# A graph layer with layer norm: the first block of M moved ahead of the c products, r on half columns, and one of the last normalisations given to VectorE

## The chip, the cores and the metric

One core of one Trainium2 chip. The metric is the device time of one execution in microseconds, the median of several runs. Names of engines: TensorE (PE; PEld are its weight loads), VectorE (DVE), ScalarE (ACT), GpSimd (POOL), and SyncE (SP), which here only issues loads and stores.

## The reference

`x` is 128 graphs of 64 nodes with 384 features (8192 tokens), `adj` a 64 x 64 matrix of 0 and 1 for each graph. Cut to what matters:

```
dep_emb = dep_emb_table[adj]
hi = x @ W1[:384] + dep_emb @ W1[384:] + b1          # for each pair i, j
hj = x @ W2[:384] + dep_emb @ W2[384:] + b2
relevance = sum(hi * hj, -1)
A = softmax(where(adj != 0, relevance, -1e9), axis=2)
h = relu((A @ x) @ gcn_w + gcn_b)
out = layernorm(x + h @ Wo + bo)
```

Where `adj` is 1 everywhere that counts, the embedding is one fixed row (type 1), so with c1 = emb[1] @ W1[384:] + b1 and c2 likewise, relevance is a bilinear form in x: x_i M x_j, with M = W1[:384] W2[:384]^T, plus x_i . u with u = W1 c2, plus x_j . r with r = W2 c1, plus k = c1 . c2. The kernel computes this, and at the end looks whether an entry of `adj` is over 1; only then does it run a second, general program, which these inputs don't need.

## The kernel before, in words

The tokens are worked in 16 groups of 512 (four tiles of 128 tokens, `q` 0 to 3). The loop over the groups is written out as a pipeline: `body(g, par)` runs for each group on every engine, the first two and the last two groups with their indices fixed. In a group TensorE mixes (`mix`, L523), forms scores (`score_stage`, L468), values of the next group (`value`), the output product of the group before (L544 to L550), a transpose (L503) and the projection of the next group (`proj`). Large products are made in three parts from a high and a low half (`three`, L444 to L446). Each engine's order is written out by hand in its own block of the program, and semaphores join them: `x.then_inc(s, 1)` raises `s` when x is done, and `wait_ge(s, n)` holds the engine, with all that is queued behind, until it has that value.

The change lies in two places. The first is the start:

- TensorE, once VectorE has cleared `zero`, multiplies zeros (`warm`, L557) with the widths in `WARM_UP`. Then it computes c1 and c2 (L569: six products from `edge_sb`, 64 columns each, into two PSUM banks), one more product of zeros of width `FILL`, and M (L579): for each of three blocks c of the sum, three products d of 128 x 385 that add into three banks. The first 384 columns are M, the last, column `HID` of `w2t_sb`, is c2, so that u comes out with M. M waits for the loads of w1 and w2 (`w12_loaded[c]`) and, ahead of block 0, for `c2_ready`.
- r follows (`r_stage`, L587): three columns of 128, each a sum of three products whose weights are 128 columns of `w2t_sb` and whose moving operand is c1, repeated over 64 columns, into `score`. Then L595 lays gcn_b out over all rows (`gb_diag` times ones, into `GB_BANK`), and the value products of group 0 begin. Behind the first of them stands the small product for k (L599).
- VectorE copies the embedding, waits for `bias_loaded` and `c_mm`, writes c2 into column `HID` of `w2t_sb` (L893), writes `c2_sb` and `c1_sb`, then `gb_diag`, c1 * c2, the low halves of x (L907) and of gcn_w (L911), u's low half (L914), and the copy of gcn_b's row (L917), then M's low halves.
- ScalarE issues the loads of the embedding, w1, the biases and gcn_w, and makes the high halves (L770 to L784). SyncE issues the loads of w2 (L378) and x. GpSimd makes the identity and part of the low halves of x.

The second place is the end, the last group (`LAST`, 15). For each of its four tiles VectorE adds x, takes the statistics (L864) and the moments (L873); GpSimd adds eps and takes the power -1/2 (`inverse_std`, L1152 and L1154); for tiles 0 to 2 GpSimd also computes the shift (`shift`, L1161) and ScalarE normalises with it (`normalise_last`, L763), after which SyncE stores the tile (L422). Tile 3 is normalised by VectorE from PSUM (L1035), and ScalarE issues its store (L828). Between its moments and that, VectorE computes the flag of the general program (L1030, L1032). `normalise` (L881) is VectorE's form from SBUF, used in the groups before.

## Time and profile before

| | us |
|---|---|
| runs | 382.44, 381.17, 382.26 |
| median | 382.26 |
| the profiled execution, its own time | 382.89 |
| its span, first to last instruction | 380.8 |
| TensorE busy in it | 373.4 |
| VectorE busy | 218.5 |
| GpSimd busy | 153.3 |
| ScalarE busy | 142.5 |

The profile is of one execution. The views used are the page (busy time of each engine, the chain of work that ended last, followed back from the last instruction), the timeline (start and length of instructions in order), the chain of waits in a stretch, the tables by source line, and the busy time by stretch with the granted clock of TensorE as a share of 2.4 GHz. Times are us from the start of the span. A product on float32 data stands as two records, a weight load and a product each; a row with "x12" merges twelve of them. In brackets stands how long the engine had stood idle, and what ended that.

### The profile page before, as it was taken

The numbers are of one execution on the slowest core, as the hardware profiler recorded it, in microseconds if no ns is written. First come the engines' busy times: TensorE is split into PE (matmuls) and PEld (weight loads), VectorE is DVE, ScalarE is ACT, GpSimd is POOL, SyncE is SP. The second block draws the span as 40 slices with busy tenths as digits, with TensorE's granted clock in tenths as the row PEclk, the third lists the DMA queues.
The fourth block names the chain that finished last, engine by engine and source line by source line (L and its number), as shares of the span: only waits on it lengthen the run. The fifth ranks groups of instructions, "written<-read, shape, count | busy, mean of one in ns | idle before, by whom it ended". The sixth has DMA issues, their size and how long they took to land.

```text
span 380.8 us, 10033 instructions
## 1 busy us (share of the span) xinstructions
PE 373.4 (98%) x3983; PEld 342.3 (90%) x3983; DVE 218.5 (57%) x582; ACT 142.5 (37%) x343; POOL 153.3 (40%) x134
## 2 busy tenths in 40 slices
PE   8999999999999999999999999999999999999993
PEld 5789898998989899898989989898998989898993
DVE  1534265665646566464756646476664647666594
ACT  1724541523434152343414234341523435133343
POOL 0332545080724508072450807235080723608034
PEclk9999999999999999999999999999999999999998
DMA  7922022608053170715317071431707143170105
GB/s 231 318 102 84 16 83 45 221 2 226 37 166 98 29 233 0 218 44 147 114 27 234 0 209 53 139 123 22 239 0 209 52 133 129 26 240 0 45 27 184
DMA packets 34851, 42.88 MB, mean 113 GB/s; under 512 B 10128, under 2 KB 29072, under 8 KB 34832
## 3 DMA queue, kind: packets, MB, share of 16 engines
q1 hardware_dynamic: 33600, 41.13, 35.7%
q10 hardware_dynamic: 1232, 1.49, 1.2%
q8 instruction: 13, 0.21, 0.2%
q14 instruction: 6, 0.05, 0.0%
HBM read 30.03 MB, written 12.58 MB: 112 GB/s over the span
## 4 chain that ended last, share of the span: by engine, by line
PE 91%; DVE 4%; DMA 1%; POOL 1%; ACT 1%; issue 0%; ACTq 0%; POOLq 0%
PE banks L444 18%; PE banks L446 18%; PE banks L445 18%; PE banks L544 7%; PE banks L550 7%; PE banks L545 7%; PE banks L523 6%; PE banks L468 6%; PE banks L579 2%; DMA bias_sb<-in_biases_dram 1%; DVE stats L864 1%; PE banks L503 1%; POOL rstd L1154 1%; DVE y_sb L859 1%; DVE hs_lo L942 1%; PE banks L587 1%
## 5 line engine op out<-in xcount | busy, mean ns | idle before, releaser
L1143 POOL TENSOR_TENSOR x_sb<-x_sb,wob_sb 128x1536 f32<-128x1536 f32 x15 | 52.8, 3519 | 175.9 <-DVE weights L973 162.8
L942 DVE SCALAR_TENSOR_TENSOR hs_lo<-banks,hs_hi 128x256 fp32r<-128x256 f32 x90 | 32.5, 416 | 67.3 <-ACT hs_hi L804 67.2
L444 PE MATMUL banks<-gcn_hi,xt_hi 128*128 128x386 f32 x192 | 66.9, 348 | 0.0
L446 PE MATMUL banks<-gcn_hi,xt_lo 128*128 128x386 f32 x192 | 64.9, 338 | 0.0
L445 PE MATMUL banks<-gcn_lo,xt_hi 128*128 128x386 f32 x192 | 64.8, 338 | 0.0
L544 PE MATMUL banks<-wo_hi,hs_hi 128*128 128x384 f32 x180 | 60.9, 338 | 0.0
L550 PE MATMUL banks<-wo_hi,hs_lo 128*128 128x384 f32 x180 | 60.5, 336 | 0.0
L545 PE MATMUL banks<-wo_lo,hs_hi 128*128 128x384 f32 x180 | 60.5, 336 | 0.0
L745 ACT ACTIVATE gt_sb<-banks,r_sb 128x512 f32<-128x512 f32 x48 | 33.0, 688 | 71.5 <-PE banks L446 71.4
L444 PE MATMUL banks<-xt_hi,m_hi 128*128 128x512 f32 x144 | 57.4, 398 | 0.0
L446 PE MATMUL banks<-xt_hi,m_lo 128*128 128x512 f32 x144 | 56.8, 394 | 0.0
L445 PE MATMUL banks<-xt_lo,m_hi 128*128 128x512 f32 x144 | 56.4, 392 | 0.0
L1134 POOL TENSOR_TENSOR xt_lo<-xt_sb,xt_hi 128x1536 fp32r<-128x1536 f32 x15 | 52.8, 3521 | 0.7 <-ACT xt_hi L739 0.7
L859 DVE TENSOR_TENSOR y_sb<-banks,x_sb 128x384 f32<-128x384 f32 x60 | 33.3, 555 | 28.4 <-PE banks L550 28.4
L849 DVE TENSOR_TENSOR hg_sb<-banks,gb_row 128x385 f32<-128x385 f32 x64 | 34.4, 554 | 23.0 <-PE banks L446 23.0
L444 PEld LDWEIGHTS banks<-gcn_hi,xt_hi 128*128 128x128 f32 x192 | 36.3, 189 | 1.2
L445 PEld LDWEIGHTS banks<-gcn_lo,xt_hi 128*128 128x128 f32 x192 | 36.3, 189 | 0.2
L794 ACT ACTIVATE prob<-rel,nmax 128x64 f32<-128x64 f32 x64 | 21.5, 337 | 39.5 <-DVE nmax L961 39.5
L446 PEld LDWEIGHTS banks<-gcn_hi,xt_lo 128*128 128x128 f32 x192 | 36.3, 189 | 0.0
L864 DVE BATCH_NORM_STATS2 stats<-y_sb 128x6 f32<-128x384 f32 x60 | 33.6, 560 | 2.0
L544 PEld LDWEIGHTS banks<-wo_hi,hs_hi 128*128 128x128 f32 x180 | 33.9, 188 | 0.2
L545 PEld LDWEIGHTS banks<-wo_lo,hs_hi 128*128 128x128 f32 x180 | 33.8, 188 | 0.1
(97 smaller groups left out, 516.0 us busy)
## 6 DMA issues: line engine op xcount, KB each, us to landing
xt_sb<-in_x_t_dram SPq DMA_DIRECT2D x15, 768.0 KB, 4.5
x_sb<-in_x_dram SPq DMA_DIRECT2D x15, 768.0 KB, 5.6
out_dram<-y_sb SPq DMA_DIRECT2D x30, 384.0 KB, 5.8
adj_sb<-in_adj_dram SPq DMA_DIRECT2D x32, 64.0 KB, 2.2
xt_sb<-in_x_t_dram SPq DMA_DIRECT2D x2, 384.0 KB, 8.4
xt_sb<-in_x_dram SPq DMA_DIRECT2D x1, 768.0 KB, 4.7
w1t_sb<-in_w_t_dram ACTq DMA_DIRECT2D x3, 192.0 KB, 5.4
w2t_sb<-in_w_t_dram SPq DMA_DIRECT2D x3, 192.0 KB, 4.5
```

Of the source, the lines that this page charges most:

```text
L444: pe.matmul(acc, a_hi, b_hi, start=first, stop=False)
L445: pe.matmul(acc, a_hi, b_lo, start=False, stop=False)
L446: return pe.matmul(acc, a_lo, b_hi, start=False, stop=last)
L544: pe.matmul(acc, hs_home(g)[0][:, c, ts], wo_hi[:, c, :], start=opens, stop=False)
L545: pe.matmul(acc, hs_home(g)[0][:, c, ts], wo_lo[:, c, :], start=False, stop=False)
L550: mm = pe.matmul(out_bank(g, q)[:, 0:HID], hs_home(g)[1][:, c, ts], wo_hi[:, c, :], start=False, stop=(c == BLOCKS[-1]))
L849: dve.tensor_tensor(hg_sb[:, slot, q, :], VALUE_BANK[q][:, 0:HID + 1], gb_row[:], ALU.add).then_inc(hg_ready, 1)
L859: dve.tensor_tensor(y_home(g, slot)[:, q, :], out_bank(g, q)[:, 0:HID], x_home(g, slot)[:, q, :], ALU.add).then_inc(added, 1)
L864: dve.bn_stats(stats[:, q, :], y_home(g, slot)[:, q, :]).then_inc(statd, 1)
L942: a = dve.scalar_tensor_tensor(by_graph(hs_home(g)[1][:, f, :])[:, h], mixed(f)[:, h], 0.0, by_graph(f32(hs_home(g)[0][:, f, :]))[:, h], A ...
L1134: pool.tensor_tensor(xt_lo[:, slot], xt_sb[:, slot], f32(xt_hi[:, slot]), ALU.subtract).then_inc(xlo, 1)
L1143: pool.tensor_tensor(x_home(g, slot), x_home(g, slot), wob_sb[:].rearrange("p (o n) -> p o n", o=1).to_broadcast([P, PAIRS, HID]), ALU.add ...
```

## The change

In words:

- `WARM_UP` becomes three products of 384 columns (were 384, 384, 128), and the filler product behind the c products goes.
- M's first block (`m_stage(0)`) comes right behind the warm-up. It waits for its loads and for `zero_column`: VectorE sets the column `HID` of block 0 of `w2t_sb` to 0 (its second instruction), so that the block adds nothing to u.
- The c products follow, then the row of gcn_b, now in bank 2. Behind them six products with one column each (weights: 64 columns of `w1t_sb` block 0; moving: `c2_sb[:, 0:1]`) add block 0's part of u into column `HID` of M's banks. They wait for both c2 writes. Then come M's blocks 1 and 2.
- r's products are cut into halves of 64 weight columns each, 18 in place of nine.
- VectorE writes `gb_diag` ahead of its wait for the c products, and copies gcn_b's row ahead of the low halves of x. As bank 2 is the second value product's, that product waits for `gb_row_ready`.
- In the last group GpSimd's shift and ScalarE's normalisation go for tile 2. VectorE normalises it from SBUF right behind tile 3's moments, ahead of the flag. SyncE's store of it and ScalarE's store of tile 3 wait for `y_ready` with the counts that belong to that.

TensorE, start of the program, before (names: `edge_sb` holds embedding and its weights, `c_sb` are c1 and c2):

```order
L557 MATMUL banks<-zero 128x384 [waits warm_zero]
L557 MATMUL banks<-zero 128x384
L557 MATMUL banks<-zero 128x128
L569 MATMUL banks<-edge_sb 128x64 [waits emb_ready,edge_loaded1,edge_loaded0]
L569 MATMUL banks<-edge_sb 128x64 x5
L557 MATMUL banks<-zero 128x128
L579 MATMUL banks<-w2t_sb,w1t_sb 128x385 [waits c2_ready,w12_loaded0]
L579 MATMUL banks<-w2t_sb,w1t_sb 128x385 x2
L579 MATMUL banks<-w2t_sb,w1t_sb 128x385 [waits w12_loaded1]
L587 MATMUL banks<-c_sb,w2t_sb 128x64 [waits c1_ready]
L587 MATMUL banks<-c_sb,w2t_sb 128x64 x8
L595 MATMUL banks<-gb_diag,ones 128x384 [waits gb_diag_ready,ones_ready]
```

The same place after the change:

```order
L560 MATMUL banks<-zero 128x384 x2
L571 MATMUL banks<-w2t_sb,w1t_sb 128x385 [waits w12_loaded0,zero_column]
L571 MATMUL banks<-w2t_sb,w1t_sb 128x385 x2
L592 MATMUL banks<-edge_sb 128x64 [waits emb_ready,edge_loaded1,edge_loaded0]
L592 MATMUL banks<-edge_sb 128x64 x5
L597 MATMUL banks<-gb_diag,ones 128x384 [waits gb_diag_ready,ones_ready]
L603 MATMUL banks<-c_sb,w1t_sb 64x1 [waits c2_ready]
L603 MATMUL banks<-c_sb,w1t_sb 64x1 x5
L571 MATMUL banks<-w2t_sb,w1t_sb 128x385 [waits w12_loaded1]
L581 MATMUL banks<-c_sb,w2t_sb 64x64 [waits c1_ready]
L581 MATMUL banks<-c_sb,w2t_sb 64x64 x17
```

M's first block has moved ahead of the c products, and between them and M's second block stand the row of gcn_b and six products of one column.

VectorE, end of the program, before:

```order
L1025 BN_STATS stats<-banks 128x6 [waits out_mm]
L873 BN_AGGR mv<-stats 128x2 [waits statd]
L1030 TENSOR_REDUCE all_max<-banks 1x1 [waits rowmax_mm]
L1032 TENSOR_SCALAR general<-all_max 1x1 [waits allmax_ready]
L1035 TENSOR_SCALAR xt_sb<-banks,mv,rstd 128x384 [waits rstd_ready]
```

and after:

```order
L1041 BN_STATS stats<-banks 128x6 [waits out_mm]
L887 BN_AGGR mv<-stats 128x2 [waits statd]
L895 TENSOR_SCALAR xt_sb<-xt_sb,mv,rstd 128x384 [waits rstd_ready]
L1047 TENSOR_REDUCE all_max<-banks 1x1 [waits rowmax_mm]
L1049 TENSOR_SCALAR general<-all_max 1x1 [waits allmax_ready]
L1052 TENSOR_SCALAR xt_sb<-banks,mv,rstd 128x384 [waits rstd_ready]
```

The row of L895 is tile 2's normalisation, and the maximum, the flag and tile 3's normalisation now stand behind it.

```diff
@@ -47,8 +47,7 @@
 P = 128
 NEG = 1.0e9
 EPS = 1e-5
-WARM_UP = 384, 384, 128
-FILL = 128
+WARM_UP = 384, 384, 384
 
 
 def gnn_layernorm_kernel(nc, x, x_t, adj, adj_t, edge, biases, w1_t, w2_t, gcn_w, wo_w, wo_b, out):
@@ -175,8 +174,8 @@
         PROJ0_BANK = bank[5:8]
         PROJ1_BANK = [bank[5], bank[2], bank[3]]
         C_BANK = bank[3], bank[4]
+        GB_BANK = bank[2]
         ROWMAX_BANK = bank[4]
-        GB_BANK = bank[4]
         BLOCKS = 0, 2, 1
         K_AT = C * NODES
 
@@ -206,6 +205,7 @@
         ident_zero = sem("ident_zero")
         ident_ready = sem("ident_ready")
         warm_zero = sem("warm_zero")
+        zero_column = sem("zero_column")
         attn_zero = sem("attn_zero")
         ones_ready = sem("ones_ready")
         c_mm = sem("c_mm")
@@ -418,7 +418,10 @@
             sp.dma_start(x_sb[:, 1], x_rows[1]).then_inc(x_loaded[1], 16)
             run(sp, body)
             for q in range(PAIRS - 1):
-                sp.wait_ge(y_end, q + 4)
+                if q < HALVES:
+                    sp.wait_ge(y_end, q + 4)
+                else:
+                    sp.wait_ge(y_ready, HALVES * (LAST - 1))
                 sp.dma_start(out_rows[LAST][:, q], y_home(LAST, 1)[:, q]).then_inc(stored[1], 16)
             again = is_general(sp)
 
@@ -561,6 +564,26 @@
             for n in WARM_UP:
                 warm(n)
 
+            def m_stage(c):
+
+                pe.wait_ge(w12_loaded[c], 32)
+                for d in range(C):
+                    mm = pe.matmul(M_BANK[d][:, 0:HID + 1], w1t_sb[:, c, d * P:(d + 1) * P], w2t_sb[:, c, :],
+                                   start=(c == 0), stop=(c == C - 1))
+                    if c == C - 1:
+                        mm.then_inc(m_mm, 1)
+
+            def r_stage(d):
+
+                for c in range(C):
+                    for e in range(2):
+                        at = d * P + e * NODES
+                        pe.matmul(score[e * NODES:(e + 1) * NODES, d * NODES:(d + 1) * NODES],
+                                  w2t_sb[:, c, at:at + NODES], c1_sb[:, c:c + 1].to_broadcast([P, NODES]),
+                                  start=(c == 0), stop=(c == C - 1))
+
+            pe.wait_ge(zero_column, 1)
+            m_stage(0)
             for n in range(2):
                 pe.wait_ge(edge_loaded[n], 16)
             pe.wait_ge(emb_ready, 1)
@@ -569,35 +592,26 @@
                     mm = pe.matmul(C_BANK[n][:, c * NODES:(c + 1) * NODES], w[:, c * P:(c + 1) * P],
                                    emb[:, 1:2].to_broadcast([EDIM, NODES]), start=True, stop=True)
             mm.then_inc(c_mm, 1)
-            warm(FILL)
-
-            for c in range(C):
-                pe.wait_ge(w12_loaded[c], 32)
-                if c == 0:
-                    pe.wait_ge(c2_ready, 1)
-                for d in range(C):
-                    mm = pe.matmul(M_BANK[d][:, 0:HID + 1], w1t_sb[:, c, d * P:(d + 1) * P], w2t_sb[:, c, :],
-                                   start=(c == 0), stop=(c == C - 1))
-                    if c == C - 1:
-                        mm.then_inc(m_mm, 1)
-
-            def r_stage(d):
-
-                for c in range(C):
-                    pe.matmul(score[:, d * NODES:(d + 1) * NODES], w2t_sb[:, c, d * P:(d + 1) * P],
-                              c1_sb[:, c:c + 1].to_broadcast([P, NODES]), start=(c == 0), stop=(c == C - 1))
-
-            pe.wait_ge(c1_ready, 1)
-            for d in range(C):
-                r_stage(d)
             pe.wait_ge(ones_ready, 1)
             pe.wait_ge(gb_diag_ready, 1)
             pe.matmul(GB_BANK[:, 0:HID], ones[:].to_broadcast([P, P]), gb_diag[:],
                       start=True, stop=True).then_inc(gb_mm, 1)
+            pe.wait_ge(c2_ready, 2)
+            for d in range(C):
+                for e in range(2):
+                    at = d * P + e * NODES
+                    pe.matmul(M_BANK[d][e * NODES:(e + 1) * NODES, HID:HID + 1], w1t_sb[:, 0, at:at + NODES],
+                              c2_sb[:, 0:1], start=False, stop=False)
+            m_stage(1)
+            m_stage(2)
+            pe.wait_ge(c1_ready, 1)
+            for d in range(C):
+                r_stage(d)
             value(0, 0, 0)
             pe.wait_ge(c12_sb_ready, 1)
             pe.matmul(score[:, K_AT:K_AT + C], ones[:].to_broadcast([P, P]), c12_sb[:],
                       start=True, stop=True).then_inc(rk_mm, 1)
+            pe.wait_ge(gb_row_ready, 1)
             value(0, 0, 1)
             pe.wait_ge(m_lo_ready, C)
             pe.wait_ge(xlo, 1)
@@ -822,9 +836,9 @@
             normalise_last(LAST - 2, 1, 1, (2, 3))
             normalise_last(LAST - 1, 0, 2, (0, 1))
             normalise_last(LAST - 1, 0, 3, (2, 3))
-            for q in range(PAIRS - 1):
+            for q in range(HALVES):
                 normalise_last(LAST, 1, q + 4, (q,))
-            act.wait_ge(y_ready, HALVES * (LAST - 1))
+            act.wait_ge(y_ready, HALVES * (LAST - 1) + 1)
             act.dma_start(out_rows[LAST][:, PAIRS - 1], y_home(LAST, 1)[:, PAIRS - 1]).then_inc(stored[1], 16)
 
             with act.If(is_general(act)):
@@ -883,24 +897,28 @@
                 a.then_inc(y_ready, 1)
 
             dve.memset(zero[:], 0.0).then_inc(warm_zero, 1)
+            dve.memset(w2t_sb[:, 0, HID:HID + 1], 0.0).then_inc(zero_column, 1)
             dve.memset(attn[:], 0.0).then_inc(attn_zero, 1)
             dve.memset(ones[:], 1.0).then_inc(ones_ready, 1)
             dve.memset(adj_max[:], 0).then_inc(max_zero, 1)
             dve.wait_ge(edge_loaded[0], 16)
             dve.tensor_copy(emb2_sb, emb1_sb).then_inc(emb_ready, 1)
             dve.wait_ge(bias_loaded, 16)
-            dve.wait_ge(c_mm, 1)
-            dve.tensor_tensor(w2t_sb[:, :, HID], C_BANK[1][:, 0:C * NODES:NODES], b2_sb, ALU.add).then_inc(c2_ready, 1)
-            dve.tensor_tensor(c2_sb[:], C_BANK[1][:, 0:C * NODES:NODES], b2_sb, ALU.add).then_inc(c2_ready, 1)
-            dve.tensor_tensor(c1_sb[:], C_BANK[0][:, 0:C * NODES:NODES], b1_sb, ALU.add).then_inc(c1_ready, 1)
             dve.memset(gb_row[:, HID:HID + 1], 0.0)
             dve.wait_ge(ident_ready, 1)
             for c in range(C):
                 a = dve.tensor_scalar(gb_diag[:, c * P:(c + 1) * P], ident[:], gb_sb[:, c:c + 1], None, ALU.mult)
             a.then_inc(gb_diag_ready, 1)
+            dve.wait_ge(c_mm, 1)
+            dve.tensor_tensor(w2t_sb[:, 1:C, HID], C_BANK[1][:, NODES:C * NODES:NODES], b2_sb[:, 1:C],
+                              ALU.add).then_inc(c2_ready, 1)
+            dve.tensor_tensor(c2_sb[:], C_BANK[1][:, 0:C * NODES:NODES], b2_sb, ALU.add).then_inc(c2_ready, 1)
+            dve.tensor_tensor(c1_sb[:], C_BANK[0][:, 0:C * NODES:NODES], b1_sb, ALU.add).then_inc(c1_ready, 1)
             dve.wait_ge(c2_ready, 2)
             dve.wait_ge(c1_ready, 1)
             dve.tensor_tensor(c12_sb[:], c1_sb[:], c2_sb[:], ALU.mult).then_inc(c12_sb_ready, 1)
+            dve.wait_ge(gb_mm, 1)
+            dve.tensor_copy(gb_row[:, 0:HID], GB_BANK[:, 0:HID]).then_inc(gb_row_ready, 1)
 
             for c in range(C):
                 dve.wait_ge(xt0_hi, c + 1)
@@ -913,8 +931,6 @@
                 dve.wait_ge(u_hi_ready, c + 1)
                 dve.tensor_tensor(gcn_lo[:, c, HID:HW], M_BANK[c][:, HID:HID + 1].to_broadcast([P, 2]),
                                   f32(gcn_hi[:, c, HID:HW]), ALU.subtract).then_inc(u_lo_ready, 1)
-            dve.wait_ge(gb_mm, 1)
-            dve.tensor_copy(gb_row[:, 0:HID], GB_BANK[:, 0:HID]).then_inc(gb_row_ready, 1)
             for d in range(C):
                 dve.wait_ge(m_hi_ready, d + 1)
                 dve.tensor_tensor(m_lo[:, d, :], M_BANK[d][:, 0:HID], f32(m_hi[:, d, :]),
@@ -1025,6 +1041,7 @@
             dve.bn_stats(stats[:, q, :], out_bank(LAST, q)[:, 0:HID]).then_inc(statd, 1)
             dve.wait_ge(statd, PAIRS * GROUPS)
             moments(LAST, (q,))
+            normalise(LAST, 1, PAIRS - 1, (2,))
 
             dve.wait_ge(rowmax_mm, 1)
             dve.tensor_reduce(all_max[:], ROWMAX_BANK[0:1, 0:P], AX_X, ALU.max).then_inc(allmax_ready, 1)
@@ -1201,7 +1218,7 @@
             run(pool, body)
             for q in range(PAIRS):
                 inverse_std(LAST, q, slice(q, q + 1))
-                if q < PAIRS - 1:
+                if q < HALVES:
                     shift(LAST, q, (q,))
 
             with pool.If(is_general(pool)):
```

## Rows read from the trace of the kernel before

**Rows 1.** The page: busy time by engine, and the chain that ended last by engine.
```profile
PE 373.4 (98%) x3983; PEld 342.3 (90%) x3983; DVE 218.5 (57%) x582; ACT 142.5 (37%) x343; POOL 153.3 (40%) x134
...
PE 91%; DVE 4%; DMA 1%; POOL 1%; ACT 1%; issue 0%; ACTq 0%; POOLq 0%
```
**Rows 2.** Chain of waits from 4 to 18.8 us: start, length, what.
```profile
1.95 4.59 DMA bias_sb<-in_biases_dram
...
6.87 7.52 PE banks L579 x18
14.39 1.95 PE banks L587 x18
16.34 0.70 PE banks L595 x2
```
**Rows 3.** Timeline of TensorE up to M: start, length, engine, line, operation.
```profile
0.92 3.35 PE L557 MATMUL banks<-zero 128*128 128x384 f32 x6 [0.92 <-DVE zero L885]
4.21 1.55 PE L569 MATMUL banks<-edge_sb 64*128 64x64 f32 x12
5.68 0.79 PE L557 MATMUL banks<-zero 128*128 128x128 f32 x2
```
**Rows 4.** Busy time and granted clock of one stretch (PEclk before the DMA share).
```profile
0.00:4.00 4.00, 3.08 (x6) 1.85 (x6) 0.90 (x5) 0.00 (x0) 0.94 (x9) 1.00 0.45 131
```
**Rows 5.** Timeline of TensorE's weight loads in M, one record each.
```profile
7.64 0.33 PEld L579 LDWEIGHTS banks<-w2t_sb,w1t_sb 128*128 128x128 f32 x1 [0.31 <-issue]
...
9.56 0.32 PEld L579 LDWEIGHTS banks<-w2t_sb,w1t_sb 128*128 128x128 f32 x1 [0.30 <-issue]
10.02 0.19 PEld L579 LDWEIGHTS banks<-w2t_sb,w1t_sb 128*128 128x128 f32 x1
10.67 0.19 PEld L579 LDWEIGHTS banks<-w2t_sb,w1t_sb 128*128 128x128 f32 x1
```
**Rows 6.** w2's loads: their issue, and the first one's time to landing.
```profile
1.52 1.63 SPq L378 DMA_DIRECT2D w2t_sb<-in_w_t_dram  x3
...
w2t_sb<-in_w_t_dram SPq DMA_DIRECT2D x1, 192.0 KB, 4.8
```
**Rows 7.** Chain of waits: the first score stage.
```profile
29.81 1.55 PE banks L468 x48
```
**Rows 8.** Weight loads of r and of a score stage, ns min/median/max.
```profile
L587 PEld LDWEIGHTS banks<-c_sb,w2t_sb x18: 190/192/192, 13.9 to 16.0; 128*128 128x128 f32 x18
...
L468 PEld LDWEIGHTS banks<-xt_sb,gt_sb x48: 132/138/138, 29.7 to 31.1; 128*64 128x64 f32 x48
```
**Rows 9.** Timeline of VectorE at the start.
```profile
11.57 1.09 DVE L907 TENSOR_TENSOR xt_lo<-xt_sb,xt_hi 128x256 fp32r<-128x256 f32 x3 [4.05 <-ACT xt_hi L770]
...
17.08 0.56 DVE L917 COPY gb_row<-banks 128x384 f32<-128x384 f32 x1 [2.07 <-PE banks L595]
```
**Rows 10.** Timeline behind the last product, on VectorE, GpSimd and ScalarE's queue.
```profile
375.22 0.18 DVE L873 BATCH_NORM_AGGREGATE mv<-stats 128x2 f32<-128x6 f32 x1
375.32 0.25 DVE L1030 TENSOR_REDUCE all_max<-banks 1x1 f32<-1x128 f32 x1
375.46 0.27 POOL L1161 TENSOR_SCALAR nmr<-mv,rstd 128x1 f32<-128x1 f32 x1
375.60 0.14 DVE L1032 TENSOR_SCALAR general<-all_max 1x1 int32<-1x1 f32 x1
375.69 0.19 POOL L1152 TENSOR_TENSOR veps<-mv,eps_sb 128x1 f32<-128x1 f32 x1
...
375.96 0.55 POOL L1154 TENSOR_TENSOR rstd<-veps,mhalf 128x1 f32<-128x1 f32 x1
376.54 0.68 DVE L1035 TENSOR_SCALAR xt_sb<-banks,mv,rstd 128x384 f32<-128x384 f32 x1 [0.80 <-POOL rstd L1154]
377.25 0.37 ACTq L828 DMA_DIRECT2D out_dram<-xt_sb  x1
```
**Rows 11.** VectorE's normalisations from SBUF, ns min/median/max.
```profile
L881 DVE TENSOR_SCALAR y_sb<-y_sb,mv,rstd x54: 446/474/480, 61.9 to 351.4; 128x384 f32<-128x384 f32 x54
```

## The prediction, made before the changed kernel was run

> **What bounds the kernel now.** I read the page first. TensorE is busy 98% of the span and the chain that ended last is 91% TensorE [rows 1], so between the first and the last product nothing but TensorE's own stream counts: time put into it or taken out of it arrives at the end. What is left is the stretch before the stream is dense and the stretch behind it. So I read the chain of waits over the first 19 us [rows 2]. It runs from the bias load, which lands at 1.95 + 4.59 = 6.54, over two small VectorE operations into M, which starts at 6.87 and lasts 7.52, then r (1.95), the row of gcn_b (0.70), and from 17.04 on the dense value products. In the timeline of TensorE ahead of it [rows 3] stand the warm-up until 4.27, the c products until 5.76 and the one filler product until 6.47: all three are spent waiting for the bias and for w2's first block, so none of them costs anything now.
>
> Then the clock. The granted clock reads 1.00 from the start [rows 4], but the records say otherwise: a product on float32 data has two records, and the weight loads of M that begin at 7.64 and 9.56 are three records apart, 0.64 us each; the next follows after 0.46, at 10.02, and two later it is 10.67, 0.32 each [rows 5]. 385 columns in 0.64 and in 0.32 are the 1.2 GHz and the 2.4 GHz level, so I go by the spacing and not by the granted clock, which has no record of the start. If the 0.46 is part slow and part fast, the rise is at 9.56 + 0.28 = 9.84. TensorE had then been busy since 0.92 but for 0.4 us ahead of 6.87, with the small c products in the middle.
>
> The tail I read in the timeline [rows 10]. VectorE's last normalisation waits for rstd, which GpSimd ends at 375.96 + 0.55 = 376.51, and GpSimd was kept by the shift of the third tile.
>
> **M's first block.** It no longer waits for the bias but for the zero column and for w1 and w2. w2's block is issued at 1.52 and lands 4.8 later, at 6.32 [rows 6]; M can start at 6.39 in place of 6.87, 0.48 earlier. The longer warm-up has two products with 256 more columns each, 0.43 us more apiece at 0.64 per 384 columns: it ends at 4.27 + 0.86 = 5.1, still ahead of 6.32, so it costs nothing, and TensorE stands idle for 1.3 us behind it. If the clock rises at 9.84 as before, the six records of the block start at 6.39, 7.16, 7.80, 8.44, 9.08 and 9.72 (first gap 0.77, as 6.87 to 7.64 before) and end at 10.10; before, the sixth ended at 10.34. **Term: -0.24.**
>
> **The c products.** Twelve records take 5.68 - 4.21 = 1.47 [rows 3]. They used to lie in the wait for the loads; now they lie behind M's first block, on the path. r's records with the same 64 columns go at the fast clock in (16.34 - 14.22) / 18 = 0.118 each, against 0.122 here, so the clock doesn't change their price; 0.1 less is the lower end. **Term: +1.47.** The filler leaves with no effect, as it was in the wait.
>
> **The row of gcn_b** moves from behind r to behind the c products: 0.65 to 0.7 either way [rows 2]. It covers most of the way from the last c product over two VectorE operations to c2, which took 0.33 between bias and M [rows 2]. Term: 0. Its copy on VectorE (0.56) now stands ahead of xt_lo (1.09 for three) [rows 9], which so start at about 13 and end at 14.2; the first value product, which wants them, comes at about 17.8. Covered by 3 us; with no cover the most is the whole 0.56. The wait of the second value product for gb_row ends 5 us before it.
>
> **The six products that add u's first block**, twelve records with one moving column and 64 weight columns: nothing like it is in the trace. Nearest is the score stage, 48 records of 64 x 64 that alternate between the two column halves, in 1.55 [rows 7], 0.032 each: 0.39. The other end is r's record now, 0.118: 1.4. Below 0.4 it can't well go, as the records must be issued on a busy engine. The form is the score stage's, so I take 0.4 and 0.1 for getting under way. **Term: +0.5**, range +0.4 to +1.4.
>
> **r on half columns.** 18 products of 64 x 64 in place of nine of 128 x 64, 36 records. At the score stage's rate 36 x 0.032 = 1.16, in place of 2.12. **Term: -0.96**; the other end is 0 or a little over, if two half products take as long as a whole one. What bounds the whole ones is that the weights of the next (0.192 alone) and a short product take turns [rows 8]. The Trainium skill (TensorE: Matmul & The Clock Gate, Part 3, on what overlaps) has weight loads overlap with running products only where the row group differs, and here every product uses all rows. By that rule column halves would win nothing over r as it is, and the sum would be 1.0 higher. The score stage alternates column halves with all rows in use and still goes at 0.032 a record while one of its weight loads lasts 0.138 [rows 7, 8]: the loads do overlap, and the row decides.
>
> Before M's end the chain over ScalarE's u_hi and VectorE's u_lo has to be ready for the first value product. Today r's 2.12 covers it, and no wait shows; with 1.16 the cover is thinner. What follows M's last product there is two ScalarE copies and two VectorE subtractions, the longest of them no longer than the 0.56 of the gcn_b copy, and they overlap in pairs; I take it to stay hidden, and give it 0.3 in the upper end.
>
> **The tail.** GpSimd leaves out the third tile's shift (0.27). The last rstd then waits for the moments of tile 3, at 375.22 + 0.18 = 375.40, in place of 375.69: veps 0.19 and rstd 0.55 with 0.16 between gives 376.3 in place of 376.51 [rows 10]. VectorE takes the third tile's normalisation, 0.47 [rows 11], ahead of the maximum and the flag (0.42 together): 375.40 + 0.47 + 0.42 = 376.3 as well. So the last normalisation starts 0.2 earlier, and with it the last store, issued at 377.25. **Term: -0.2**, range -0.3 to +0.2 (VectorE the later one). The third tile's own store goes out earlier, at about 375.9, and is not last.
>
> **Sum:** -0.24 + 1.47 + 0.5 - 0.96 - 0.2 = +0.57. The profiled execution took 382.89 (span 380.8), so its like would take 383.46. That execution is 0.63 above the median of the runs shown, 382.26; on the median I forecast **382.8**. A measurement of this kernel can tell about 0.3%, 1.15 us, from no change; the forecast lies inside.
>
> **Rivals.**
> 1. *The clock rises before M's first block.* The warm-up is now one piece of full-width products until 5.1, where it ended at 4.27 and the small c products followed. If that brings the clock up, the block's six records take 6 x 0.32 and some 0.1, 2.0 in place of 3.71: 1.7 less, **381.1**. For it: the three runs shown spread over 1.27 us, about the price of some slow records, as if the rise fell differently in them. Against it: the 1.3 us of idle behind the warm-up, and that nearly unbroken work from 0.92 to 6.47 did not bring it up before M in the trace [rows 3, 5]. The spread of the runs weighs enough for a chance of 0.35. The Trainium skill (the same page, Part 1, on what is happening) calls the point of the rise variable from run to run, because the monitor does not start with the kernel; the spread would agree, and one trace alone can't show it.
> 2. *The clock rises later.* The c products and the u products, small in columns, now stand in the middle of M. If they break up the activity before the rise, the row of gcn_b (0.65 more) and three records of M's second block (0.32 more each) go at the slow level: +1.6, **384.4**. It decides when the rise would otherwise have come after 10.1. Against it: M's first block is dense from 6.39 on, as M was from 6.87 when the clock rose at 9.84. Chance 0.10.
> 3. *Column halves don't run side by side.* r costs 2.1 as now, and u's records 0.118 each: 0.96 + 0.9 more, **384.7**; with r alone, 383.8. Against it stand the 48 records of the score stage. Chance 0.08.
> 4. The forecast's own case, rise at about 9.84: 0.47.
>
> **How the numbers follow.** Rival 1 at 381.1 lies just at the bound of 0.3% (381.1), and with the scatter of a median some two thirds of it is told as faster: 0.23, and 0.04 for a cheaper path than I see: faster 0.27. Slower (above 383.4) are rivals 2 and 3 and a tenth of the forecast's case, where u or the tail are at their upper ends: 0.23. The rest, 0.50, is within 0.3%. The range 380.8 to 384.0 takes in rival 1 with some scatter, the forecast's case with u at its upper end (+0.9), and r alone without a gain; outside are most of rival 2 and the whole of rival 3. The forecast's own case spans 382.2 to 383.8.
>
> **What would show it.** M's first weight load at 6.35; its records 0.64 apart until about 9.8, or 0.32 from the start (rival 1); c products from about 10.1; M's second block at 12.7 (its loads have landed by then); r in 1.2; the first value product at 17.8 in place of 17.04; the end of TensorE's stream 0.8 later; the last normalisation 0.2 nearer to the last product. I am wrong in the mechanism if the value products start before 17.0 with the clock rising at 9.8 or later, or if r takes more than 1.6.

## The result, and the profile after

| | us |
|---|---|
| changed kernel, six runs | 379.76 to 380.41, median 379.96 |
| kernel before, six runs beside it | 381.17 to 383.34, median 382.31 |
| ratio | 0.9944, 95% interval 0.9924 to 0.9964 |
| the changed kernel's profiled execution, its own time | 380.05 |
| its span | 378.0 |

The change makes the kernel faster by 0.56%, about 2.1 us. I had forecast 382.8 with a range of 380.8 to 384.0: no change, where there is a clear gain, and 379.96 lies below the range.

The page of the changed kernel, busy time and the chain, against [rows 1]:

```profile
PE 372.1 (98%) x4011; PEld 340.0 (90%) x4011; DVE 220.7 (58%) x584; ACT 142.1 (38%) x342; POOL 153.3 (41%) x133
...
PE 98%; DVE 0%; POOL 0%; issue 0%
```

The chain is now TensorE's from the warm-up on: no load and no VectorE operation bounds the start of this execution. The chain of waits from 3 to 18 us, against [rows 2]:

```profile
2.56 2.56 PE banks L560 x4
5.12 2.79 PE banks L571 x6
7.91 0.81 PE banks L592 x12
8.72 0.84 PE banks L597 x2
9.56 0.45 PE banks L603 x12
10.01 4.08 PE banks L571 x12
14.09 1.20 PE banks L581 x36
15.29 0.38 PE banks L447
```

In this order stand the warm-up, M's first block, the c products, the row of gcn_b, u's six products, M's other blocks, r, and the first value product at 15.29, where it was at 17.04. So the value products begin 1.75 us earlier. About 0.2 of that is lost at once, as the first of them takes 0.38 where it took 0.17; TensorE's last product starts 1.66 earlier (374.42 before, 372.76 after). That is the start's part of the difference of 2.8 between the two spans. The weight loads of M's first block, against [rows 5]:

```profile
5.00 0.50 PEld L571 LDWEIGHTS banks<-w2t_sb,w1t_sb 128*128 128x128 f32 x2 [1.03 <-issue]
5.81 0.33 PEld L571 LDWEIGHTS banks<-w2t_sb,w1t_sb 128*128 128x128 f32 x1 [0.31 <-issue]
6.45 0.20 PEld L571 LDWEIGHTS banks<-w2t_sb,w1t_sb 128*128 128x128 f32 x1 [0.31 <-issue]
6.78 0.19 PEld L571 LDWEIGHTS banks<-w2t_sb,w1t_sb 128*128 128x128 f32 x1
```

5.81 to 6.45 is 0.64, the 1.2 GHz level; 6.45 to 6.78 is 0.33, the 2.4 GHz level. The clock rose at about 6.45, not at 9.84.

The other 1.2 us lies behind the last product. The timeline of the tail, against [rows 10]:

```profile
373.57 0.18 DVE L887 BATCH_NORM_AGGREGATE mv<-stats 128x2 f32<-128x6 f32 x1
373.77 0.48 DVE L895 TENSOR_SCALAR xt_sb<-xt_sb,mv,rstd 128x384 f32<-128x384 f32 x1
...
374.10 0.56 POOL L1171 TENSOR_TENSOR rstd<-veps,mhalf 128x1 f32<-128x1 f32 x1
...
374.47 0.14 DVE L1049 TENSOR_SCALAR general<-all_max 1x1 int32<-1x1 f32 x1
374.69 0.68 DVE L1052 TENSOR_SCALAR xt_sb<-banks,mv,rstd 128x384 f32<-128x384 f32 x1
375.40 0.37 ACTq L842 DMA_DIRECT2D out_dram<-xt_sb  x1
```

From the moments to the last normalisation it is 1.12 (373.57 to 374.69), where it was 1.32: the 0.2 of the forecast. But from the issue of the last store to the end of the span it is 2.6, where it was 3.55. The transfers from that issue on, before and then changed: in each the bandwidth in 40 slices, the queues that carry instructions, and the last store with its time to landing.

```profile
GB/s 0 266 369 430 328 328 369 348 144 41 0 321 287 307 348 369 389 328 267 171 0 0 0 20 0 20 0 0 20 0 20 20 20 20 21 0 0 0 0 0
...
q8 instruction: 1, 0.02, 2.0%
...
out_dram<-xt_sb ACTq DMA_DIRECT2D x1, 192.0 KB, 3.1
```

```profile
GB/s 354 354 402 307 190 24 0 0 0 0 0 0 0 165 307 354 378 378 354 354 378 189 142 0 24 126 252 0 0 0 0 0 0 0 0 0 0 0 0 0
...
q8 instruction: 1, 0.02, 2.4%
...
out_dram<-xt_sb ACTq DMA_DIRECT2D x1, 192.0 KB, 2.1
```

Before, the store's data are almost all moved by the twentieth slice (1.5 us behind the issue), and then, after a gap, single rows (20 GB/s in a slice) follow for some 0.9 us. In the changed kernel that trickle is missing. A packet of instructions, 16 KB, stands beside the store in both. Its place is what the first group of experiments turns on.

### The profile page after: what moved, and what is told of

Read it like the earlier page. It is cut to its first block, busy times and chain, and to the rows that moved or that the text cites. A ratio compares the mean times of both kernels' runs of the same rounds, so it can differ in the third digit from the quotient of the medians.

```text
span 378.0 us, 10088 instructions
## 1 busy us (share of the span) xinstructions
PE 372.1 (98%) x4011; PEld 340.0 (90%) x4011; DVE 220.7 (58%) x584; ACT 142.1 (38%) x342; POOL 153.3 (41%) x133
## 4 chain that ended last, share of the span: by engine, by line
PE 98%; DVE 0%; POOL 0%; issue 0%
PE banks L447 18%; PE banks L449 18%; PE banks L448 18%; PE banks L547 9%; PE banks L548 9%; PE banks L553 9%; PE banks L526 7%; PE banks L471 7%; PE banks L571 2%; PE banks L560 1%; PE banks L506 1%; PE banks L581 0%; PE banks L597 0%; PE banks L592 0%; DVE xt_sb L1052 0%; PE banks L540 0%
## 6 DMA issues: line engine op xcount, KB each, us to landing
out_dram<-y_sb SPq DMA_DIRECT2D x30, 384.0 KB, 5.8
xt_sb<-in_x_t_dram SPq DMA_DIRECT2D x2, 384.0 KB, 8.4
```

## The experiments

Sixteen kernels ran, in four series, each on another chip. The kernel before was timed 29 to 35 times in each series. These times fall into two groups: in the first series 16 from 380.45 to 381.47 and 13 from 382.09 to 382.95, in the others 17, 20 and 20 in the lower one and 18 (from 381.94), 15 (from 382.31) and 14 (from 382.01) in the upper. I call them its early and its late group; the part on the start says why.

| kernel | median | of the kernel before, same series | ratio (95% interval) |
|---|---|---|---|
| after_old_tail | 381.36 | 381.23 | 0.9996 (0.9981 to 1.0011) |
| after_whole_r | 380.39 | 381.23 | 0.9977 (0.9958 to 0.9995) |
| after_short_warm | 381.23 | 381.23 | 0.9984 (0.9963 to 1.0005) |
| after_again | 379.57 | 381.94 | 0.9949 (0.9930 to 0.9968) |
| after_c_first | 379.55 | 381.94 | 0.9946 (0.9923 to 0.9968) |
| after_flag_first | 381.00 | 381.94 | 0.9974 (0.9955 to 0.9994) |
| before_long_warm | 381.39 | 381.94 | 1.0002 (0.9981 to 1.0024) |
| before_flag_last | 380.99 | 381.28 | 0.9972 (0.9948 to 0.9995) |
| before_new_tail | 379.69 | 381.28 | 0.9968 (0.9947 to 0.9989) |
| before_half_r | 380.71 | 381.28 | 0.9972 (0.9953 to 0.9991) |
| after_flag_last | 379.92 | 381.28 | 0.9965 (0.9941 to 0.9989) |
| after_third | 380.05 | 381.16 | 0.9969 (0.9947 to 0.9991) |
| start_only | 381.99 | 381.16 | 1.0012 (0.9990 to 1.0034) |
| after_longer_warm | 380.24 | 381.16 | 0.9966 (0.9947 to 0.9984) |
| row_loaded | 379.28 | 381.16 | 0.9947 (0.9924 to 0.9969) |

before_again was one execution, 380.75. The median of a kernel with two groups jumps with a few runs from one to the other, so I compare groups where I can.

### The tail

**after_old_tail.** The changed kernel with the tail of before:

```diff
-            normalise(LAST, 1, PAIRS - 1, (2,))
...
-                if q < HALVES:
+                if q < PAIRS - 1:
                     shift(LAST, q, (q,))
```

with ScalarE's normalisation of tile 2 and the waits of the two stores as before.

> The changed kernel with the tail of before (ScalarE normalises tile 2 behind GpSimd's shift). Theory A (in the tail the change wins only the 0.2 us by which the last normalisation comes nearer to the last product; that the last store landed 1.0 us sooner behind its issue is chance): 380.2, 0.2 over the changed kernel's 380.0. Theory B (the store lands sooner because the stores before it went out sooner): 381.1, and the last store takes 3.1 us to land again.

Measured: 381.36, and the last store takes 3.1 again. The three series that have the changed kernel have it at 0.9944, 0.9949 and 0.9969 of the kernel before; without the new tail it is at 0.9996. So the tail is worth 1.0 to 2.0 us, not 0.2, and the store's landing is no chance. Theory B of this run had the effect right but named the wrong cause, as the next runs show.

**after_flag_first and before_flag_last.** The same four lines (the maximum over `adj` and the flag of the general program), moved in opposite directions:

```diff
+            dve.tensor_scalar(general[:], all_max[:], 1.0, None, ALU.is_gt).then_inc(general_ready, 1)
             normalise(LAST, 1, PAIRS - 1, (2,))
```

is the first, the changed kernel with the flag ahead of tile 2. The second is the kernel before with the flag behind tile 3:

```diff
                               ALU.subtract, ALU.mult).then_inc(y_ready, 1)
+            dve.tensor_scalar(general[:], all_max[:], 1.0, None, ALU.is_gt).then_inc(general_ready, 1)
```

> The changed kernel with the maximum and the flag ahead of tile 2's normalisation on VectorE, as early as in the kernel before. Theory A (an instruction load of 16 KB follows the flag by 2.3 to 2.8 us in every trace so far; with the early flag it falls into the last store's packets and holds up the last nine of them): the last store takes 3.1 us to land in place of 2.1, and the median is 0.7 to 1.0 above the changed kernel. Theory B (the store lands sooner because tile 2's store went out sooner): 2.1 again, and no difference.

> The kernel before with the maximum and the flag moved behind tile 3's normalisation on VectorE; nothing else. Theory A (the load of instructions that follows the flag is what holds up the last store): the last store lands 2.0 to 2.1 us behind its issue in place of 3.1 to 3.6, and the median is 0.8 to 1.3 below the kernel before, with its two groups still there. Theory B (the new tail's gain needs tile 2's earlier store): 3.1 again, no difference.

Measured: after_flag_first has its runs from 380.56 to 381.52, median 381.00, 1.4 above the changed kernel of the same series. Its last store and the transfers behind 375.5:

```profile
GB/s 355 410 341 355 137 0 146 0 0 68 259 341 396 355 192 27 73 0 14 14 0 14 14 14 27 14 0 0 0 0 0 0 0 0 0 0 0 0 0 0
...
out_dram<-xt_sb ACTq DMA_DIRECT2D x1, 192.0 KB, 3.1
```

The trickle is back, with tile 2's store as far ahead of the last one as in the changed kernel: its issue ends 0.79 us before the last one's begins in both. In before_flag_last the trickle is gone, and tile 2's store is as close to the last one as in the kernel before (0.42 in both):

```profile
GB/s 382 369 205 301 369 328 410 314 55 0 0 0 0 287 410 369 341 287 55 0 273 355 341 396 301 82 0 0 0 0 0 0 0 146 73 0 0 0 0 0
...
out_dram<-xt_sb ACTq DMA_DIRECT2D x1, 192.0 KB, 1.9
```

Its four lowest runs are 379.43 to 379.85, where the early group of the kernel before begins at 380.49, and the other eight are 380.97 to 381.56, where the late group begins at 382.31: both groups are lower, by 1.1 and 1.3 at their lowest runs. The flag's place alone is worth that. The packet of instructions says how: it starts 2.34 us behind the flag in the kernel before (375.74 to 378.08) and 2.51 in the changed one (374.61 to 377.12), and 2.0 to 2.8 in all traces. Before, this falls into the store's packets, here with the last column the share of the sixteen engines' time in 0.2 us:

```profile
q8 instruction: 1, 0.02, 30.0%
q10 hardware_dynamic: 13, 0.02, 26.7%
```

(the kernel before, 378.0 to 378.2), while in the changed kernel, from 377.0 to 377.2, one packet of the store is left:

```profile
q8 instruction: 1, 0.02, 30.6%
q14 instruction: 1, 0.01, 15.8%
q10 hardware_dynamic: 1, 0.00, 0.2%
```

The share gives the packet's length: 30.0% of sixteen times 0.2 us is 0.96 us. So in the kernel before the instruction packet is done at 379.04, and the last rows of the store begin at 379.03. The same holds in all seven traces with an early flag: the last eight rows begin to move within 0.02 us of the packet's end, and the store lands 1.3 us behind that end. Where the packet took longest (before_long_warm, 44.8% of 0.2 us, so 1.43 us), the store did too, 3.6. Over all eighteen traces, the store lands 3.1 to 3.6 behind its issue in the seven with an early flag, and 1.9 to 2.2 in the eleven with a late one. That some engine of the DMA handles both and serves them in turn is what I conclude from these times; the traces don't name the engine.

**before_new_tail.** The kernel before with the four edits of the new tail.

> The kernel before with the changed tail alone. Theory A: the flag is late enough as a side effect, the store lands in 2.0 to 2.1, and the last normalisation comes 0.2 nearer: 1.0 to 1.5 below the kernel before, two groups still there. Theory B (the tail is worth the 0.2 that I forecast): 0.2 below.

Measured: eight runs from 378.78 to 379.94 and four from 381.19 to 381.84, the groups 1.7 and 1.1 below those of the kernel before at their lowest runs, with the store at 2.0. Theory A. The new tail is worth about 1.3: in the traces 1.1 of it is the store's landing (3.1 to 2.0), the side effect that VectorE comes to the flag later, and 0.2 the effect that I had priced. The runs can't tell that 0.2 from nothing: before_flag_last, which lacks it, is as far below the kernel before (ratios 0.9972 and 0.9968).

**after_flag_last.** The changed kernel with the flag behind tile 3's normalisation.

> The changed kernel with the flag behind tile 3's normalisation. Theory A (the later load of instructions is clear of the store by more, but the branch over the general program ends later by about 0.7): the store lands in 2.0 to 2.1 as in the changed kernel, and the time is within 0.3 of it. Theory B (the flag ahead of the last normalisation costs VectorE time on the path): 0.2 to 0.5 below the changed kernel.

Measured: nine runs from 379.16 to 380.26, three from 381.80 to 382.30. The changed kernel did not run in this series; in the others its lower runs lie from 379.16 to 380.84, and so do these nine. The store lands in 1.9. No more shows than with the flag between the two normalisations. Theory A.

### r

**after_whole_r and before_half_r** exchange the halved products of r for the whole ones, in the changed kernel and in the one before:

```diff
-                    for e in range(2):
-                        at = d * P + e * NODES
-                        pe.matmul(score[e * NODES:(e + 1) * NODES, d * NODES:(d + 1) * NODES],
+                    pe.matmul(score[:, d * NODES:(d + 1) * NODES], w2t_sb[:, c, d * P:(d + 1) * P],
```

> The changed kernel with r on whole columns again. Theory A (36 records in 1.20 us side by side in place of 18 in 2.12, all of it on the path): 380.9, 0.9 more. Theory B (r covers the chain to u's low half, or something behind it waits anyway): 380.0 to 380.4.

> The kernel before with r on half columns alone. Theory A (on the path in full): r takes 1.2 in place of 2.1 and the median falls by 0.9. Theory B (the row of gcn_b or u's low half, which r covered, is waited for instead): 0.2 to 0.6 less, and an idle stretch of TensorE behind r.

Measured: whole r has 11 of 12 runs from 379.92 to 380.75, median 380.39, a ratio of 0.9977 against 0.9944 to 0.9969 for the changed kernel: 0.3 to 1.3 us more. Half r in the kernel before gives 380.71 to 381.28, ratio 0.9972. Here the late group comes down by the full 0.8 (its lowest runs 381.52, against 382.31), but the early one by 0.4 only (380.06 against 380.49). The trace suggests why the halves differ. It is an early execution, and M ran into its own loads, as the chain of waits from 4 us on has it:

```profile
2.43 6.62 DMA w1t_sb<-in_w_t_dram
...
9.09 4.15 PE banks L579 x12
13.24 1.20 PE banks L589 x36
```

r itself takes 1.20 in place of 1.95 to 2.1. The wait that appears is not B's, but one for w1's second block, which landed 6.6 us behind its issue in this trace; one trace doesn't show how often that happens. Nor is the price quite Theory A's 0.9. In the chain r gets 0.75 shorter (1.95 to 1.20), the row of gcn_b behind it 0.14 longer (0.70 to 0.84), and from M's end to the second value product it is 0.62 less than in the kernel before (2.83 to 2.21). The traces of after_whole_r and the changed kernel differ by 0.60 in the same stretch. So r is worth about 0.6.

### The start and the clock

**before_again**, the kernel before unchanged:

> The kernel before, unchanged, for a second trace. Theory A (two loads landed late by chance in the first trace, w2's first block 4.8 us and the bias 4.6 us behind their issue, where the changed kernel's trace has 3.4 and 3.1): here they land about 3.3 behind their issue again in many executions, M starts near 5.9, behind the filler product, and the time is about 381.3. Theory B (the landing belongs to the kernel's own order of work): M starts at 6.87 again, and the time is about 382.5.

Measured: 380.75, and a chain that differs from [rows 2] in two ways:

```profile
1.94 3.91 DMA bias_sb<-in_biases_dram
...
6.18 6.06 PE banks L579 x18
12.24 1.95 PE banks L587 x18
...
14.90 0.18 PE banks L444
```

The bias landed 0.7 earlier, so theory A is half right: the landing varies. The more important difference is that M takes 6.06 in place of 7.52. Its weight loads and those of the c products:

```profile
4.19 0.97 PEld L569 LDWEIGHTS banks<-edge_sb 64*128 64x128 f32 x12 [0.23 <-issue]
...
6.15 5.47 PEld L579 LDWEIGHTS banks<-w2t_sb,w1t_sb 128*128 128x128 f32 x18 [0.62 <-DMA w2t_sb<-in_w_t_dram]
```

18 loads in 5.47 are 0.32 apart from the first: the clock was up before M, from the c products on (0.97 for twelve where it was 1.36). Without any change in the code the first value product comes at 14.90 in place of 17.04. These are the two groups. The traces of the kernel before and of its variants bear it out: the clock is up before M in before_again (380.75), before_new_tail (379.10) and before_half_r (380.92), all in the lower group of their kernel; it rises only in M's first block, at 9.5 or later, in the first trace (382.89), before_flag_last (381.19) and before_long_warm (383.65), all in the upper one. The Trainium skill (TensorE: Matmul & The Clock Gate, Part 1, on what is happening) says that the point of the rise varies from run to run. The six traces agree, but not with the page's size of it, 500 ns either way: by the spacing of the records the clock is up by 4.1 us in before_new_tail, and not before 9.7 in before_long_warm.

**before_long_warm.** The longer warm-up and no filler product, in the kernel before:

```diff
-WARM_UP = 384, 384, 128
-FILL = 128
+WARM_UP = 384, 384, 384
```

> The kernel before with the longer warm-up (three times 384) and without the filler product. Theory A (the length of the dense stretch sets how often the clock rises before M): the slow group of the kernel before, near 382.5, thins out or goes, and the median comes down by about 0.5 or more. Theory B (only the order with M's block behind the warm-up does it): both groups stay as they are.

Measured: 381.39, ratio 1.0002, three of twelve runs at 383.16 or more, where the kernel before has 18 of 35 in its late group. With twelve runs that is a hint of fewer late rises, no proof. Its late runs are later still: its trace has M from 7.03, and the loads 0.64 apart until 9.73.

**after_short_warm.** The changed kernel with the old warm-up, 384, 384, 128.

> The changed kernel with the warm-up of before (384, 384, 128 columns). Theory A (the longer warm-up is what brings the clock up at 6.5, in the middle of M's first block): with 0.86 us less of it the rise comes a good deal later, all six records of the first block, the c products, the row of gcn_b and part of the second block run at the slow level, 381.5 to 382.5. Theory B (the rise follows from M's first block coming early and close behind the warm-up, and not from the warm-up's length): 380.0, with M at 5.0 either way.

Measured: two groups again, five runs from 379.55 to 380.16 and seven from 381.00 to 382.19. Five are as good as the changed kernel; the others are late. The trace is one of those:

```profile
5.95 0.33 PEld L571 LDWEIGHTS banks<-w2t_sb,w1t_sb 128*128 128x128 f32 x1 [0.31 <-issue]
6.59 0.34 PEld L571 LDWEIGHTS banks<-w2t_sb,w1t_sb 128*128 128x128 f32 x1 [0.31 <-issue]
...
7.88 0.34 PEld L571 LDWEIGHTS banks<-w2t_sb,w1t_sb 128*128 128x128 f32 x1 [0.30 <-issue]
```

M's first block starts at 5.18, as in the changed kernel, and runs at the slow level nearly to its end. TensorE had stood idle for 0.9 us from 4.27 on. Theory A: with the shorter warm-up seven of twelve runs are late, and B is out, as M began equally early. The whole set of kernels with the changed start and the long warm-up (the changed kernel, after_old_tail, after_whole_r, after_flag_first, after_flag_last and start_only) has 8 late runs of 90. The run doesn't tell whether the longer work counts or the smaller gap behind it, for both changed. A gap need not cost the clock: in start_only the warm-up ended at 4.58, TensorE waited 1.62 us for w2, and M's first block ran at the fast level throughout:

```profile
6.20 2.18 PE L568 MATMUL banks<-w2t_sb,w1t_sb 128*128 128x385 f32 x6 [1.62 <-DMA w2t_sb<-in_w_t_dram]
```

**after_longer_warm.** Four warm-up products.

> The changed kernel with four warm-up products in place of three: the fourth ends at 6.4 at the slow level, or at 5.8 to 6.1 where the clock has risen by then. Theory A (the rise needs dense work ahead of it and what is lost is the delay of M's first block): no slow run, narrower scatter, M's first block at 5.8 to 6.4 mostly at the fast level, and a median 0 to 0.6 above the changed kernel. Theory B (the rise does not depend on the warm-up): 0.8 to 1.3 above, the whole delay of M.

Measured: 379.27 to 380.90, median 380.24, against 380.05 for after_third beside it, which has two runs at 382.15 and 382.16. No late run, and 0.2 more. Theory A. Twelve runs without a late one are no proof against 8 of 90, and the intervals of the two kernels overlap.

**after_again and after_third**, the changed kernel unchanged:

> The changed kernel, unchanged, beside the others of this call. Theory A (the clock's rise falls differently in each execution, and a dense warm-up until 5.1 lets it fall between about 4.5 and 7.0 every time): runs within 1 us of one another, no second group, while the kernel before falls into two groups about 1.7 us apart. Theory B (the change moves one fixed rise): both kernels scatter alike. The median is about 1.2 below the kernel before of the same call by either; the last store lands 2.1 us behind its issue.

> The changed kernel once more, as the measure for the other three of this call: about 379.6 to 380.0, with at most one run in twelve 1.5 or more above the rest.

Measured: 379.16 to 380.47 in twelve runs, then ten from 379.32 to 380.84 and two at 382.15. With the first six that is 2 late runs of 30, where the kernel before had 60 of 133 in the four series. I had expected none in the first of the two and at most one in the second; the second has two.

**after_c_first.** The c products ahead of M's first block, all else as changed:

```diff
-            pe.wait_ge(zero_column, 1)
-            m_stage(0)
...
             mm.then_inc(c_mm, 1)
+            pe.wait_ge(zero_column, 1)
+            m_stage(0)
```

> The changed kernel with the c products ahead of M's first block, all else as changed. Theory A (the c products cost 1.47 us when they run ahead of the rise and 0.81 behind it, and small products put off the rise in part of the runs): M's first block starts at about 6.6, the median is 0.5 to 1.0 above the changed kernel, and some runs are 1.5 above the rest. Theory B (c products cost the same anywhere, and w2's first block often lands at 5.7 or later, so that they fill a wait): equal to the changed kernel within 0.3.

Measured: ten runs from 378.75 to 379.80 and two at 381.40 and 381.75, median 379.55, the same as the changed kernel's 379.57. Its lowest run is 0.4 below the changed kernel's, but the ten lower runs have the same median. w2's block lands anywhere from 3.3 to 4.8 us behind its issue over the traces, and the c products can fill a wait for it. The median is B's; the two late runs would be A's, but 2 of 12 can't be told from 2 of 30. So M's first block ahead of the c products is not what the gain rests on. A start without a wait for the bias is common to both orders; whether it matters, start_only tells.

**start_only.** The changed start with r whole and the old tail.

> The changed start alone: warm-up, M's first block, c products and u's products as changed, r on whole columns and the old tail. Theory A (the start wins by keeping the clock's rise early, and nothing by its own work): the fast runs equal the early group of the kernel before of the same call, near 381.0, or lie up to 0.5 above it, and the late group near 382.6 is missing or thin; the median is 0 to 0.7 below the kernel before. Theory B (the start wins because M no longer waits for the bias): also below the early group of the kernel before, by 0.4 or more.

Measured: ten runs from 381.29 to 382.47, two at 383.95 and 384.06, median 381.99. The kernel before of the same series has 20 runs from 380.01 to 381.50 and 14 from 382.01 to 383.03. So the new start alone lies between the groups, ratio 1.0012 (0.9990 to 1.0034). The chain of its trace:

```profile
1.52 4.54 DMA w2t_sb<-in_w_t_dram
...
6.20 2.18 PE banks L568 x6
8.37 0.81 PE banks L586 x12
9.19 0.84 PE banks L591 x2
10.03 0.45 PE banks L597 x12
10.48 4.08 PE banks L568 x12
14.56 1.95 PE banks L576 x18
16.51 0.24 PE banks L444
```

Here the clock is up before M as in before_again, M starts at the same time (6.20 and 6.18), and yet the first value product comes at 16.51 in place of 14.90. The 1.6 between are the c products (0.81), u's products (0.45), and the seams at M's restart and the row of gcn_b (0.3 together). Both theories fall: the median is no lower than before's, and the ten lower runs are about 1.0 above its early group (medians 381.84 and 380.79). Of A only the thin late group is left. The new start takes about 1.0 (runs) to 1.6 (the two traces) longer in a good execution, and is spared most of the bad ones.

**row_loaded.** The changed kernel with gcn_b's row loaded by one broadcast load on SyncE's queue in place of the product, the diagonal and the copy; c2's products stand ahead of c1's, and VectorE makes c2 while c1's run.

```diff
+            sp.dma_start(gb_row[:, 0:HID], gcn_b.to_broadcast([P, HID])).then_inc(gb_row_ready, 16)
...
-            pe.matmul(GB_BANK[:, 0:HID], ones[:].to_broadcast([P, P]), gb_diag[:],
-                      start=True, stop=True).then_inc(gb_mm, 1)
```

> Meant to beat both: the changed kernel with the row of gcn_b loaded over all rows by one load in place of TensorE's product and VectorE's diagonal and copy, and c2's products ahead of c1's so that VectorE makes c2 under c1's products. Theory A (the row's 0.84 is on the path, c2's way of 0.55 then shows by 0.1 to 0.2): the value products start 0.6 to 0.75 earlier and the median is 0.5 to 0.8 below the changed kernel. Theory B (w1's second and third block, which land 5.4 to 6.0 behind their issue, at 8.3 to 8.5, are then waited for, and the new load delays others): 0 to 0.3 below.

Measured: 379.28, ratio 0.9947, against 380.05 and 0.9969 for after_third in the same series; one of its eleven runs is late (381.61). The chain of waits:

```profile
8.08 1.08 PE banks L593 x12
...
9.21 0.52 PE banks L600 x12
9.72 4.08 PE banks L572 x12
```

Between the end of M's first block and M's second it is 1.64 now (8.08 to 9.72), where it was 2.10 (7.91 to 10.01): 0.46 less, where 0.6 to 0.75 was expected. The row's 0.84 is gone, but the c products in their new order take 1.08 in place of 0.81. By the medians it is 0.8 less, the lowest median of its series, but its interval overlaps after_third's, so the gain is likely and not shown.

## Why the prediction was wrong

**The tail's term, -0.2, failed.** The step is "the last normalisation starts 0.2 earlier, and with it the last store": it took the store's 3.1 us to landing as fixed. The 0.2 came as forecast (1.12 in place of 1.32), but moving the normalisation of tile 2 ahead of the flag moved the flag, too, by about 0.7 against the last store, and with it the instruction load. The term measured -1.3 (before_new_tail; by its ratio -0.4 to -2.0). I had counted what VectorE does ahead of the flag as time on VectorE alone, and had not asked what else follows the flag.

**The sum was taken from one execution that stood in the late group.** The step that failed is "if the clock rises at 9.84 as before": in the changed kernel's trace it rose at 6.45. I carried the late trace to the median by a shift of 0.63, as though all runs were alike, though the runs spread over 1.27. Rival 1 had the mechanism (the clock before M's first block, most of its cost gone) with a chance of 0.35. It happens in about half the runs of the kernel before already, which I had not seen, and in 28 of 30 of the changed one the run is in the lower group. Against it I had put the idle time of 1.3 us behind the warm-up. In the changed kernel's trace there was none: w2's block landed 3.4 behind its issue, not 4.8, and M followed the warm-up at 5.03. And where there was one, of 1.3 us in row_loaded and 1.6 in start_only, the clock was up already. The start's terms without r came to +1.73 (-0.24, +1.47, +0.5); start_only has +0.5 by its ratio (-0.4 to +1.3), so they missed by about as much as the tail's.

**The c products, +1.47.** "The clock doesn't change their price" was wrong. I compared 0.122 for a record of 64 weight rows at the slow level with 0.118 for one of r at the fast level; behind the rise the twelve take 0.81, 0.068 each.

**Right:** r's own time (1.16 forecast, 1.20 measured), u's six products (0.5 and 0.45), the chain to u's low half stays hidden, and VectorE's new order costs nothing. r's term of -0.96 was too large all the same: the 2.12 that it starts from counts 0.17 in which r's first record ran beside M's last product, the chain has 1.95 to 1.20, and about 0.6 of it arrives at the second value product. The Trainium skill (TensorE: Matmul & The Clock Gate, Part 3, on what overlaps) has weight loads overlap with running products only where the row group differs. By that rule r would have gained nothing; the 36 records of column halves at 0.033 each, all on the same rows, speak against it, as the score stage had.

**The sum of the two traces' starts:** M starts 1.75 earlier (6.87 to 5.12), its first block takes 2.79 in place of 3.47 (-0.68), the c products +0.81, the row of gcn_b +0.14, u +0.45, M's other blocks +0.03 (4.05 to 4.08), r -0.75 (1.95 to 1.20): -1.75, which is 17.04 to 15.29. 1.3 of it is that w2's block landed sooner than in the trace of before. That is luck of the two executions: over all traces that block lands 3.3 to 4.8 behind its issue, whatever the kernel. In the median the parts are the tail 1.3, r about 0.6, and the start 0 to +0.5 (start_only's interval takes in no change): its work is 1.0 to 1.6 longer, against a late rise that has all but gone. They add up to 1.4 to 1.9 less; measured are 1.2 to 2.1 by the three ratios of the changed kernel.

What stays open: why 2 of 30 runs are late all the same, as none of them was traced; what in the start keeps the late rise away, the warm-up's length, the gap behind it or M's early block; and how much of the 0.2 to 0.5 us of scatter between the series is the chips'.

## What to carry to other kernels

Take more than one trace of the kernel before, or look at the list of its runs for groups, before a trace's waits are summed: two executions of this kernel differ by 2.1 us at the first value product with no change in the code. Measure the length of the warm-up by the share of late runs and not by one trace: 0.85 us less of it here brought seven late runs in twelve. But don't pay for it with longer real work: the new start alone gained nothing. And where a flag or a branch leads to other code near the end of a program, set it so that the load of instructions which follows doesn't meet the last store.

## What the runs showed of the hardware

- A 16 KB load of instructions starts 2.0 to 2.8 us behind the flag that releases the branch, lasts 0.96 to 1.43 us, and where it begins within 1 us of the store's issue, it holds up the last eight rows of that store: 3.1 to 3.6 us to landing in place of 1.9 to 2.2.
- TensorE's clock rises at a different time in each execution of the same program: ahead of the end of the c products (5.2) in one trace of the kernel before, at 9.84 in another. With the warm-up until 5.1 and M's first block behind it 2 runs in 30 are late (8 in 90 over all kernels with that start), in place of 60 in 133; with the warm-up until 4.27 and the same order it is 7 in 12.
- The granted clock has no record of the start: it reads 1.00 there while the records stand 0.64 us apart.
- 64 x 64 products on float32 data in alternate column halves take 0.033 a record, with all rows in use; with one moving column 0.038.
- The same 192 KB load lands 3.3 to 4.8 us behind its issue at the start of the program, and w1's second block once 6.6.
